# Two split products of stacked rows in place of one zero padded float32 product, in the first layer's low rank output

## What is computed

```python
logits = flat @ router_w.T                      # 4 experts, the best 2 kept
gates = jax.nn.softmax(sparse, axis=-1)
mid = jnp.einsum('tf,erf->ter', flat, A)        # 4 experts of rank 16: 64 columns
all_deltas = jnp.einsum('ter,eor->teo', mid, B) * LORA_SCALE
delta = jnp.einsum('te,teo->to', gates, all_deltas)
x = x + gb * delta
```

## Time and profile before

| | |
|---|---|
| three runs | 1899.41, 1900.38 (median), 1903.45 us |
| profiled execution | 1903.59 us |
| its span, first to last instruction | 1901.8 us |
| busy share PE, PEld, DVE, ACT, POOL | 97%, 81%, 79%, 47%, 45% |
| mean granted TensorE clock | 0.990 of full speed |
| the stage `projections1` | about 1349 to 1536 us of the span |

### The profile page before, as it was taken

How to read it: one execution, slowest core, us unless ns; L and a number is a source line. 1 busy time by engine, 2 the same in 40 slices (tenths; PEclk the granted TensorE clock), 3 DMA queues, 4 the chain that set the end, 5 groups by cost and what they waited for, 6 DMA issues and landing times.

```text
span 1901.8 us, 38226 instructions
## 1 busy us (share of the span) xinstructions
PE 1845.8 (97%) x12792; PEld 1542.3 (81%) x12792; DVE 1507.3 (79%) x2398; ACT 885.1 (47%) x2246; POOL 864.8 (45%) x870
## 2 busy tenths in 40 slices
PE   8999979999999999999999999999999989999997
PEld 5788968888888888888888888887898856666786
DVE  4677678788888888888888888788889658889887
ACT  3333334444444444444444444456555356667343
POOL 0133364444444444444444444354576646666011
PEclk9999989999999999999999999999999989999999
DMA  9677741111111111111111111222387776554121
GB/s 360 204 245 243 250 137 50 51 50 50 46 43 45 50 50 50 50 44 42 46 50 50 50 50 42 90 94 70 115 241 225 232 229 188 163 165 120 39 67 61
DMA packets 202713, 211.41 MB, mean 111 GB/s; under 512 B 19178, under 2 KB 172778, under 8 KB 201868
## 3 DMA queue, kind: packets, MB, share of 16 engines
q1 hardware_dynamic: 201124, 208.49, 35.5%
q10 hardware_dynamic: 1512, 1.90, 0.3%
HBM read 128.40 MB, written 73.53 MB: 106 GB/s over the span
## 4 chain that ended last, share of the span: by engine, by line
PE 69%; issue 12%; DVE 8%; SPq 4%; POOL 4%; DMA 2%; ACT 1%; DVEq 0%; POOLq 0%; ACTq 0%
PE ps L1140 18%; PE ps L1101 17%; PE ps L1114 7%; PE ps L1129 5%; PE ps L1152 4%; SPq L1413 3%; PE ps L1124 3%; POOL k_rot L637 2%; PE ps L2688 2%; PE ps L2724 2%; DVE f_neg_max L2101 2%; PE ps L2282 1%; PE ps L2309 1%; PE ps L2313 1%; PE ps L2236 1%
## 5 line engine op out<-in xcount | busy, mean ns | idle before, releaser
L1140 PE MATMUL ps<-wo,ot 128*128 (+1 forms) x1536 | 380.4, 396 | 0.0
L1140 PEld LDWEIGHTS ps<-wo,ot 128*128 128x128 f32 x1536 | 280.4, 189 | 54.7
L888 ACT ACTIVATE prob<-ps,neg_max 128x128 f32<-128x128 f32 (+1 forms) x512 | 208.2, 419 | 132.8 <-DVE neg_max L975 110.6
L1101 PE MATMUL ps<-ht_hi,wq 128*128 (+1 forms) x1024 | 253.2, 389 | 1.3 <-DVE q_swap L940 0.9
L1054 POOL TENSOR_TENSOR q_rot<-q_rot,q_swap 128x512 f32<-128x512 f32 x128 | 166.9, 1304 | 178.6 <-DVE q_swap L940 178.6
L895 ACT ACTIVATE pt<-ps 128x512 fp32r<-128x512 f32 x192 | 108.0, 598 | 274.6 <-PE ps L1152 274.5
L1101 PEld LDWEIGHTS ps<-ht_hi,wq 128*128 128x128 f32 x1024 | 192.0, 188 | 41.8 <-issue 1.3
L1048 POOL TENSOR_TENSOR prob<-prob,inv_sum 128x512 f32<-128x512 f32 x64 | 66.6, 1041 | 273.7 <-DVE inv_sum L984 273.7
L1114 PE MATMUL ps<-pt,vv 128*128 128x512 f32 x576 | 144.0, 394 | 4.5 <-issue 3.9
L955 DVE TENSOR_TENSOR ot<-ps,ot 128x512 fp32r<-128x512 f32 x128 | 88.3, 691 | 74.5 <-ACT ot L905 74.5
L2101 DVE TENSOR_REDUCE f_neg_max<-ps 128x4 f32<-128x512 f32 (+1 forms) x128 | 116.8, 953 | 33.5 <-PE ps L2227 26.3
(11 more groups left out here) (255 smaller groups left out, 4053.4 us busy)
## 6 DMA issues: line engine op xcount, KB each, us to landing
stack_dram<-e_part SPq DMA_DIRECT2D x192, 128.0 KB, 2.4
v_dram<-v_part SPq DMA_DIRECT2D x32, 512.0 KB, 5.9
k_dram<-k_part SPq DMA_DIRECT2D x64, 256.0 KB, 2.6
kk<-k_dram SPq DMA_DIRECT2D x128, 128.0 KB, 2.1
vv<-v_dram SPq DMA_DIRECT2D x128, 128.0 KB, 2.1
f_q<-stack_dram SPq DMA_DIRECT2D x124, 104.0 KB
f_k<-stack_dram SPq DMA_DIRECT2D x124, 104.0 KB
wmod<-in_wmod SPq DMA_DIRECT2D x12, 1024.0 KB, 14.6
```

What stands on the lines that cost most here:

```text
L888: nc.scalar.activation(p[:, h], sc[:, h], ACT.Exp, bias=neg_max[:, t, h:h + 1], accum_out=row_sum[:, t, h:h + 1]).then_inc(p_exp, 1)
L1101: mm = nc.tensor.matmul(ps_q[j][:], w[:, at:at + HD0], r[:, bass.ds(b, 2), k], start=(n == 0), stop=(n == len(passes) - 1))
L1140: mm = nc.tensor.matmul(ps_y[j][:], o[:, j, h * P:(h + 1) * P], w[:, bass.ds(at + h * D, D)], start=(n == 0), stop=(n == len(passes) - 1))
```

## The change

The factor is no longer padded. It is loaded twice, once for each half of the 128 rows (`e_b0_raw`), and split into a first part (`e_b0_hi`, ScalarE) and a rest (`e_b0_lo`, POOL). The transposed rows are copied to `e_midt_raw`. For each tile a tile of 128 rows is made: ScalarE copies that tile's 64 rows, rounded, to their own place, and VectorE writes their rest into the other 64 rows. So one product of 128 rows with `e_b0_hi` adds first part by first part and rest by first part, and a second one with `e_b0_lo` adds first part by rest and rest by rest. The MEMSET of `b0` goes. And `heads` begins with the first part of the normed rows alone, and waits for the rest in front of the ninth product.

```diff
-    b0 = at("e_b0", [2 * ER, TT, D], low(5))
+    b0_raw = at("e_b0_raw", [2 * ER, D], low(5))
+    b0 = [at("e_b0_hi", [2 * ER, D], low(5) + D * 4, F32R), at("e_b0_lo", [2 * ER, D], low(5), F32R)]
...
-    midt = small("e_midt", [TT * ER, P])
+    midt_raw = small("e_midt_raw", [TT * ER, P])
+    midt = [small(f"e_midt{t}", [2 * ER, P], F32R) for t in range(TT)]
...
     def sync_middle(sp, v):
-        if v == U0 - 2:
-            sp.wait_ge(b0_zero, 1)
-            for t in range(TT):
-                sp.dma_start(b0[t * ER:(t + 1) * ER, t], io["b0"]).then_inc(tab_in, 16)
+        pass
...
         if v == U0 - 3:
+            for half in range(2):
+                sp.dma_start(b0_raw[half * ER:(half + 1) * ER], io["b0"]).then_inc(tab_in, 16)
             sp.wait_ge(x1_step, 2)
             sp.dma_start(own[:], io["own1"]).then_inc(own_in, 16)
...
     def lora_in_out(act, b):
         act.wait_ge(m_done, b + 1)
         if b:
+            act.wait_ge(m_lo, 2 * b)
+        nc.scalar.activation(midt_raw[:], ps_m(b), ACT.Identity).then_inc(m_out, 1)
+
+    def lora_in_hi(act, b):
+        act.wait_ge(m_out, b + 1)
+        if b:
             act.wait_ge(d_done, b)
-        nc.scalar.activation(midt[:], ps_m(b), ACT.Identity).then_inc(m_out, 1)
+        for t in range(TT):
+            rows = slice(t * ER, (t + 1) * ER)
+            nc.scalar.activation(midt[t][rows], midt_raw[rows], ACT.Identity).then_inc(m_hi, 1)
...
         if v == U0 - 3:
             routed_exp(act, 0)
+            act.wait_ge(tab_in, 32)
+            nc.scalar.activation(b0[0][:], b0_raw[:], ACT.Identity).then_inc(b0_hi, 1)
...
+    def lora_in_rest(dve, b):
+        for t in range(TT):
+            rows, other = slice(t * ER, (t + 1) * ER), slice((1 - t) * ER, (2 - t) * ER)
+            dve.wait_ge(m_hi, 2 * b + t + 1)
+            nc.vector.tensor_tensor(midt[t][other], midt_raw[rows], f32(midt[t][rows]), ALU.subtract).then_inc(m_lo, 1)
...
         def step(b, slot):
+            if b < B - 1:
+                lora_in_rest(dve, b + 1)
             rotate(b, 0, 0)
...
             pool.wait_ge(keep.first_q_done, queried(v))
-            nc.gpsimd.memset(b0[:], 0.0).then_inc(b0_zero, 1)
             pool.wait_ge(mid_ready, 1)
+            pool.wait_ge(b0_hi, 1)
+            nc.gpsimd.tensor_tensor(b0[1][:], b0_raw[:], f32(b0[0][:]), ALU.subtract).then_inc(b0_lo, 1)
             residual(pool, 2)
...
     def lora_out(pe, b):
-        pe.wait_ge(m_out, b + 1)
+        pe.wait_ge(m_lo, 2 * b + 2)
         if b:
             pe.wait_ge(x2_step, 2 * b - 1)
         for t in range(TT):
-            mm = nc.tensor.matmul(ps_d(b)[:, t], midt[:], b0[:, t], start=True, stop=True)
+            for i in range(2):
+                mm = nc.tensor.matmul(ps_d(b)[:, t], midt[t][:], b0[i][:], start=not i, stop=bool(i))
...
-                pe.wait_ge(h_lo, b + 1)
+                pe.wait_ge(h_hi, b + 1)
...
+                    if n == c == g == 0 and j == 2 * KT:
+                        pe.wait_ge(h_lo, b + 1)
```

More of the change, by code:

```diff
@@ L1281, in projections1, with small @@
     small_at = [low(2)]
-    def small(name, shape):
-        tile = at(name, shape, small_at[0])
+    def small(name, shape, dt=F32):
+        tile = at(name, shape, small_at[0], dt)
         small_at[0] = -(-(small_at[0] + 4 * math.prod(shape[1:])) // 32) * 32
@@ L1359, in projections1 @@
     qkv_lo = sem("d_qkv_lo")
-    b0_zero = sem("e_b0_zero")
+    b0_hi = sem("e_b0_hi_out")
+    b0_lo = sem("e_b0_lo_out")
     v_zero = sem("e_v_zero")
@@ L1379, in projections1 @@
     m_out = sem("e_m_out")
+    m_hi = sem("e_m_hi")
+    m_lo = sem("e_m_lo")
     d_done = sem("e_d_done")
@@ L1554, in scalar_middle @@
         if v == U0 - 2:
+            lora_in_hi(act, 0)
             root(act, 0, 1)
@@ L1609, in step @@
                 lora_in_out(act, b + 1)
+                lora_in_hi(act, b + 1)
             else:
@@ L1716, in vector_normed @@
     def vector_normed(dve, v):
+        if v == U0 - 2:
+            lora_in_rest(dve, 0)
         if v == U0 - 1:
@@ L1894, in tensor_end @@
         if v == U0 - 2:
-            pe.wait_ge(tab_in, 32)
+            pe.wait_ge(b0_lo, 1)
             lora_out(pe, 0)
```

## The result

The changed kernel takes 1923.15 us (median of 4 runs, 1920.21 to 1923.42) against 1901.91 for the kernel before in the same comparison (4 runs, 1899.41 to 1903.48): a ratio of 1.0108 [1.0094, 1.0121]. It is slower by 21.2 us, where 1906.8 was forecast. The profiled execution has a span of 1921.2 us, 19.4 more than before.

The account below looks back on a forecast made before the run. TensorE was taken as the bound in the early steps, with VectorE some 2.5 us behind. Terms of 2.9 + 1.2 + 0.4 + 0.95 + 1.0 = 6.45 us on a median of 1900.4 gave 1906.8 us, range 1899.5 to 1912.

Parts of the forecast that it names:

- Slower had 0.68: Chance of a time from 1904.2 us up: 0.53 from the main case and 0.15 from a rival.
- the hold that was named: A VectorE subtraction with two SBUF inputs does its work only when the running POOL operation is over.
- Element 1's own term of 2.9: At element 1 the subtractions wait for POOL's weight split (L1800) to end; TensorE loses 2.9 us.
- The second subtraction loses again: Rival: a POOL residual operation slips between the two subtractions; elements 2 and 5 lose 2.4 us more each; 1911.6 us, chance 0.15.
- 0.4 + 0 + 0 + 0.95: Terms of elements 2 to 5: L1829's hold costs 0.4 us at element 2, 0.95 at 5; elements 3 and 4 nothing.
- Elements 3, 4, 6, 7: 0: They lose as much or gain up to 0.5 us each, and the gate waits take that up: 0.
- The gate waits of 1.71 and 1.45 us: At elements 4 and 7 `gate_lora` waits for its gate row; these waits were to remain, somewhat shorter.
- The clock behind that gap: +1.2: After TensorE's standstill at element 1 it runs partly at 1.2 GHz: 1.2 us lost, bounds 0 and 1.6.
- Element 0: +1.0: Splitting the factor makes POOL's residual late and the subtractions may be held: 1.0 us, between -0.1 and +2.
- That saves 0.78 us an element: Four split products take 0.95 us against 1.73 for a float32 pair; 6.2 us in all eight, 3.1 at most on the chain.
- `heads` waiting for h_hi: 0: `heads` waiting for h_hi in place of h_lo gains 0; at element 5 TensorE next waits for the product's input anyway.

Follow-up runs that it names:

- x1: Changed kernel with the rests of elements 1 to 7 read from PSUM, so each subtraction has one SBUF input: 1906.24 us, ratio 1.0013 to the kernel before.
- x2: Changed kernel with POOL waiting for the coming element's two subtractions before it begins the residual: 1913.41 us, ratio 1.0053 to the kernel before.
- x4: Changed kernel with 12 extra, overwritten TensorE products in the gap before the products of elements 1 to 5: 1919.02 us, ratio 1.0081 to the kernel before.
- x6: Changed kernel with only element 0's factor prepared earlier (loads, ScalarE's split, POOL's subtraction): 1920.55 us, ratio 1.0087 to the kernel before.
- x10: x9 with the clearing of `e_values` moved from VectorE to POOL: 1903.07 us, ratio 1.0003 to the kernel before.
- x11: Kernel before with only the clearing of `e_values` moved from VectorE to POOL: 1901.02 us, ratio 0.9988.
- x5: x1 with element 0's factor also prepared earlier: 1902.64 us, ratio 0.9994 to the kernel before.
- x8: Kernel before with only `heads` waiting for `h_hi`, and for `h_lo` in front of the ninth product: 1902.91 us, ratio 0.9996.
- x9: x5 with ScalarE taking the first parts of elements 1 to 7 from PSUM too: 1902.51 us, ratio 0.9998 to the kernel before.
- x13: x9 with each 512-column normalization operation on VectorE cut into two, of 255 and 257 columns: 1939.92 us, ratio 1.0186 to the kernel before.
- x3: Changed kernel with POOL waiting for element 1's two subtractions before it takes the last weight's rest: 1919.30 us, ratio 1.0078 to the kernel before.

## Why the prediction was wrong

**Direction and mechanism: right.** Slower had 0.68, and by the hold that was named. At element 1 the pair ended 0.47 us behind the POOL operation, TensorE stood still for 3.75 us, and x1 shows that the second SBUF input is the cause. Element 1's own term of 2.9 came out: its step is 5.5 us longer, and 2.6 of these are the clock's, as worked out below.

**"The second subtraction loses again": a rival, and the main term missed.** It was given 0.15 and priced for elements 2 and 5 alone. It happened at all of elements 2 to 5, for POOL's order is the same there: a 2.34 us residual operation stands right behind L1856, and each time it went between the two subtractions. This is the step that failed: the prediction let a pair pay for one POOL operation, 0.4 + 0 + 0 + 0.95 = 1.35 us for these four elements, and their steps lost 2.5, 4.4, 1.5 and 3.3, which is 11.7. x2, which takes the residual away from there, shortens the stage by 8.9 us, the clock's part at elements 3 and 5 included.

**"Elements 3, 4, 6, 7: 0": failed.** The gate waits of 1.71 and 1.45 us stood at elements 4 and 7 alone. At element 3 none was there to take up a gap of 3.31 us with the clock's 1.6 behind it, and 1.71 cannot take up element 4's 3.01. Steps 2 and 3 (elements 3 and 4) lost 4.4 and 1.5 us; the end of the pair, no longer the gate row, decides there, and the two gate waits, which were said to remain, are gone. Elements 6 and 7, without a residual behind them, came out near 0 (0.3) and below (-1.2, of which 0.9 is a wait for the second norm that is gone).

**"The clock behind that gap: +1.2": mis-sized.** It was counted for one gap with a bound of 1.6. It came behind three gaps. Before, a step without a wait takes 22.31 us from `heads` to `heads` (steps 1 and 2); now steps 1, 3 and 5 take 21.80 with the wait taken off, and those of elements 1, 3 and 5 take 2.6, 1.6 and 1.6 us more than that: 5.8 in all, as x4 gives.

**"Element 0: +1.0": too low**, outside its bound of 2. It was 2.6 us. The mechanism stood in the text (the factor's split delays POOL's residual); that TensorE's idle 0.95 us and the cheaper product would take up most did not hold. POOL's normalization began at 1301.57 and not at 1300.6, since VectorE held L1821 for 0.85 us, for which the prediction had no term. x6 takes the whole of it back.

**"That saves 0.78 us an element": right without a wait, 0.51 with one.** In x10 TensorE does not wait at element 1. From one `heads` to the next it is 4.66 us there, and 5.44 in x11, which has the float32 products in the same place:

```profile
1347.71 3.10 PE L1952 MATMUL ps<-e_hs,qkv_w 128*128 128x256 f32 x24
1350.65 0.39 PE L1898 MATMUL ps<-e_b_hi,e_midt 128*128 128x512 f32 x1
...
1352.37 6.00 PE L1952 MATMUL ps<-e_hs,qkv_w 128*128 128x256 f32 x48
```

```profile
1347.17 3.10 PE L1919 MATMUL ps<-e_hs,qkv_w 128*128 128x256 f32 x24
...
1352.61 5.99 PE L1919 MATMUL ps<-e_hs,qkv_w 128*128 128x256 f32 x48
```

Where TensorE waits, the gain is smaller even with the wait taken off: at element 3 it is 5.45 us before (1394.09 to 1399.54) and 4.94 in x5 (1395.88 to 1401.20, less its 0.38 of waiting), a saving of 0.51. The stop takes the other 0.27: the products start 3.11 us behind `heads` in place of 2.94, the wait taken off, and the first of them takes 0.50 us in place of 0.39.

**"`heads` waiting for h_hi: 0": as far as runs can tell, right** (x8).

Put together with what was measured: TensorE's waits of 17.5 us and the clock's 5.8, less 7 x 0.51 = 3.6 and the 3.4 us by which the seven steps before were longer than without waits (2.2 of it stands in the brackets of the timeline), make 16.3, by which the stage grew. With element 0's 2.6 that is the loss, but for 0.5 us of the 19.4 between the two traces.

**Why the gain did not come even without holds:** in x5 TensorE's waits in the stage are 6.5 us against 2.2 before, 5.0 of them for the subtractions, which come in VectorE's order behind its normalization. That takes what the products save. Of the 5.0, 2.56 fall to element 5, where the transposed rows come late too; that VectorE's order sets the smaller ones is argued from x9, where they stay though ScalarE's copy is gone, and not shown by an earlier VectorE.

## What to carry to other kernels

Before an operation is put on VectorE beside a busy POOL, count its SBUF inputs: one operand read from PSUM, where the data already stands, took back 17 to 18 of the 21 us here, with no other change. A small operation that is held waits for the end of the neighbour's running one, and a second in a row can wait for a second, so look at what POOL does next, not only at what it does now. A cheaper product gains only what the engine in front of it lets through: the way from the transpose to the product has to shrink with it.

## What the runs showed that was not expected

In these traces VectorE and POOL take turns, operation by operation, where both have such work queued: four pieces of 255 and 257 columns lasted as long as the four POOL operations beside them (5.29 us against 5.17, x13), and cutting an operation in two nearly doubled its cost (1.49 us in the median for the whole in x9, 1.36 for each piece). The normalization is held so though only one of its inputs is a whole tensor in SBUF: 0.54 us at the least and 1.50 in the median in the kernel before. Of the kernel before and of x13 (least, median and most, in ns):

```profile
L1664 DVE TENSOR_SCALAR d_xn<-x_stream,d_mv,d_rstd x30: 543/1496/1676, 1266.8 to 1498.2; 128x512 f32<-128x512 f32 x30
```

```profile
L1684 DVE TENSOR_SCALAR d_xn<-x_stream,d_mv,d_rstd x60: 402/1361/4585, 1266.1 to 1534.8; 128x255 f32<-128x255 f32 x30, 128x257 f32<-128x257 f32 x30
```

The Trainium skill (SBUF — State Buffer, "Who interferes with whom") lets such an operation contend only in a mode that takes both ports. No row names the mode in which these ran, but the least durations speak for a faster one: from 256 to 512 columns they rise by 0.14 us, an estimated 0.55 ns a column, where an operation on two tensors rises by about 1.0 (0.29 us for 128 columns in the earlier trace rows, 0.68 for 512 of L1754).

In the changed kernel a stop of TensorE was followed by a lower clock at elements 1, 3 and 5 (3.75, 3.31 and 3.31 us), and not at elements 2 and 4 (3.01 us each). The length of the stop alone does not decide it. At element 5 a stop of 3.49 us had no low clock behind it in x2, and one of 3.01 us had one in x3, where the next 48 products of `heads` took 7.07 us:

```profile
1453.71 0.50 PE L1895 MATMUL ps<-e_b_hi,e_midt 128*128 128x512 f32 x1 [3.49 <-DVE e_midt L1709]
...
1455.54 5.99 PE L1949 MATMUL ps<-e_hs,qkv_w 128*128 128x256 f32 x48
```

```profile
1459.55 0.50 PE L1895 MATMUL ps<-e_b_hi,e_midt 128*128 128x512 f32 x1 [3.01 <-DVE e_midt L1709]
...
1461.87 7.07 PE L1949 MATMUL ps<-e_hs,qkv_w 128*128 128x256 f32 x48
```
